# Attention scores from one stacked product of 96 rows instead of three products with a block-diagonal operand

## The reference

```python
x = x + attn(lstm(x, cond))        # LSTM over 128 steps, then causal attention, 16 heads, latent keys of 32
x = x + moe(gru(x, cond))          # GRU over 128 steps (a projection after every 4th), then 8 experts, top 2

# attention, with h the LSTM's output:
q      = einsum('bld,dhk->blhk', h, Wq)
latent = h @ Wkv_down                                  # [.., 32]
k, v   = latent @ Wk_up, latent @ Wv_up
a      = softmax(where(mask, q @ k.T / sqrt(64), min))
y      = (a @ v) @ Wout
```

## Time and profile before

| | |
|---|---|
| median of 3 runs | 546.38 us (544.72 to 546.54) |
| the profiled execution | 542.14 us, its span 540.4 us |
| TensorE busy | 508.1 us, 94% (7464 products) |
| VectorE busy | 435.9 us, 81% |
| ScalarE busy | 364.7 us, 67% |
| GpSimd busy | 34.6 us, 6% |
| query transfers | 256 of 16 KB, median 1.9 us from issue to landing |
| granted TensorE clock | 0.971 of full speed |

### The profile page before, as it was taken

One profiled execution on the slowest core, in us unless ns is written; L12 is line 12 of the kernel. 1 busy time (PEld: TensorE's weight loads), 2 busy tenths in 40 slices (PEclk: granted clock), 3 DMA queues, 4 the chain that ended last, 5 costly groups with the idle time before them and its releaser, 6 DMA issues.

```text
span 540.4 us, 20477 instructions
## 1 busy us (share of the span) xinstructions
PE 508.1 (94%) x7464; PEld 468.7 (87%) x7506; DVE 435.9 (81%) x2370; ACT 364.7 (67%) x1329; POOL 34.6 (6%) x89
## 2 busy tenths in 40 slices
PE   7988889898799999999999999999999999889997
PEld 3756666898689999999999999999999998879986
DVE  4567888789878888888888888898888888865785
ACT  2355645875467767677777777676767677776995
POOL 7000010100000000001010101010000001000010
PEclk9799999999769999999999999999999999979999
DMA  8910102010101011110101010101010111100000
GB/s 212 366 18 7 20 2 23 2 19 11 21 3 16 9 15 16 16 12 12 19 14 16 7 18 15 21 3 19 15 16 8 14 16 16 12 1 1 13 6 13
DMA packets 75121, 14.35 MB, mean 27 GB/s; under 512 B 71412, under 2 KB 74112, under 8 KB 74639
## 3 DMA queue, kind: packets, MB, share of 16 engines
q1 hardware_dynamic: 74566, 11.96, 12.3%
q10 hardware_dynamic: 456, 1.08, 0.7%
HBM read 7.78 MB, written 1.05 MB: 16 GB/s over the span
## 4 chain that ended last, share of the span: by engine, by line
PE 78%; DVE 10%; ACT 6%; issue 4%; SPq 1%; DMA 1%; POOL 0%; ACTq 0%; DVEq 0%; POOLq 0%
PE pH L516 19%; PE pY L516 13%; PE pG L516 12%; PE pL L516 9%; PE pC L516 7%; PE pV L516 7%; PE pC L608 6%; PE pS L516 5%; ACT hid L912 2%; ACT PThi L901 1%; SPq L436 1%; DVE w1lo L1189 1%; DVE ghi L1233 1%; DMA gscale<-in_gscale 1%; ACT P L895 1%
## 5 line engine op out<-in xcount | busy, mean ns | idle before, releaser
L912 ACT ACTIVATE hid<-pH,b 128x256 f32<-128x256 f32 (+1 forms) x320 | 115.1, 449 | 0.0
L516 PE MATMUL pY<-w,hid 128*128 128x128 f32 (+1 forms) x656 | 80.9, 268 | 0.0
L516 PE MATMUL pH<-ghi,w1hi 128*128 128x256 f16 (+1 forms) x320 | 76.0, 254 | 2.3 <-ACT hid L912 1.7
L516 PE MATMUL pH<-ghi,w1lo 128*128 128x256 f16 (+1 forms) x320 | 76.3, 255 | 0.0
L516 PE MATMUL pH<-glo,w1hi 128*128 128x256 f16 (+1 forms) x320 | 76.3, 255 | 0.0
L516 PEld LDWEIGHTS pY<-w,hid 128*128 128x128 f32 (+1 forms) x656 | 70.5, 171 | 0.1
L923 ACT ACTIVATE gT<-pG 128x32 f32<-128x32 f32 x128 | 24.9, 194 | 54.8 <-PE pG L516 52.8
L901 ACT ACTIVATE PThi<-pC 128x512 f16<-128x512 f32 x64 | 38.1, 596 | 22.0 <-PE pC L608 21.8
L516 PE MATMUL pG<-gRZ,gW 128*128 128x16 f32 x256 | 45.6, 254 | 4.2 <-DVE gRZ L1206 3.9
L516 PEld LDWEIGHTS pG<-gRZ,gW 128*128 128x128 f32 x256 | 40.0, 196 | 8.0 <-DVE gRZ L1206 6.8
L516 PEld LDWEIGHTS pL<-hhi,lWhi 128*128 128x128 f16 x512 | 42.1, 116 | 5.4 <-DVE hhi L1250 4.6
(11 more groups left out here) (188 smaller groups left out, 1641.0 us busy)
## 6 DMA issues: line engine op xcount, KB each, us to landing
w<-in_w SPq DMA_DIRECT2D x2, 2048.0 KB, 13.7
qbd<-qh SPq DMA_DIRECT2D x256, 16.0 KB, 1.9
out<-acc SPq DMA_DIRECT2D x16, 64.0 KB, 1.6
xT<-in_xT ACTq DMA_DIRECT2D x1, 960.0 KB, 7.9
hid<-in_WqT SPq DMA_DIRECT2D x1, 512.0 KB, 5.4
hid<-in_Wout SPq DMA_DIRECT2D x1, 512.0 KB, 9.9
lWh<-in_lWh SPq DMA_DIRECT2D x1, 256.0 KB, 2.8
lWx<-in_lWx SPq DMA_DIRECT2D x1, 256.0 KB, 3.3
```

Source lines behind the costliest of these rows:

```text
L516: return nc.tensor.matmul(o, lhsT=lhsT, rhs=rhs, start=start, stop=stop, skip_group_check=True)
L912: A(hid[:, e % NHID, c, 0:W], pH[half][:, W * at:W * (at + 1)], ACT.Gelu, bias=b1[:, e, c:c + 1], scale=1.0 / SP).then_inc(gelu, 1)
```

## The change

The three products of a sequence become one. The high and low queries and a second copy of the high queries are stacked in 96 partitions of a new tile `qst` (rows 0 to 31 high, 32 to 63 low, 64 to 95 high again), and the latents in `latst` (rows 0 to 63 `lathi`, 64 to 95 `latlo`), so that one product over 96 rows gives the same sum. No row of another head group is in it, so nothing is block-diagonal and nothing need be cleared. `qst` has two buffers, by period.

SP fills rows 0 to 63 by 8 transfers of 32 KB for each period, four from the high part and four from the low part. Rows 64 to 95 are filled by copies on the engines, in the step after the queries: two of 32x512 on ScalarE, two on VectorE. GpSimd makes two more copies a period, of 64x128 and 32x128, for `latst`. The query tile `qh` has its high and low halves apart instead of interleaved by sequence.

```diff
-            def spread_queries(n):
-                p, u = divmod(n, NU)
-                if u == 0:
-                    sp.wait_ge(q_lo, p + 1)
-                if n == 0:
-                    sp.wait_ge(cleared, NCLEAR)
-                if n >= 2:
-                    sp.wait_ge(s_mm, n - 1)
-                for q in range(HQ):
-                    r = slice(32 * q, 32 * q + 32)
-                    sp.dma_start(qbd[r, n % 2, :, :, q, :]..., qh[r, p % 2, 4 * u:4 * u + 4, :, :, :]...).then_inc(qbd_done[n % 2], 16)
+            def spread_queries(p):
+                for r, l, ready in ((0, 0, q_hi), (1, 1, q_lo)):
+                    sp.wait_ge(ready, p + 1)
+                    if p >= 2 and r == 0:
+                        sp.wait_ge(s_mm, NU * (p - 1))
+                    for q in range(HQ):
+                        sp.dma_start(qst[LD * r:LD * (r + 1), p % 2, :, 32 * q:32 * q + 32],
+                                     qh[32 * q:32 * q + 32, p % 2, l, :, :, :]...).then_inc(qst_done[p % 2], 16)
...
+                if latents_at(k - 1) is not None:          # SP, at the head of its step k
+                    spread_queries(latents_at(k - 1))
...
                 pool.wait_ge(lat_split, 2 * G + 2)
+                pool.tensor_copy(latst[0:2 * LD, :, c], lathi[0:2 * LD, :, c]).then_inc(lat_stack, 1)
+                pool.wait_ge(lat_stack, 2 * G + 1)
+                pool.tensor_copy(latst[2 * LD:3 * LD, :, c], latlo[2 * LD:3 * LD, :, c]).then_inc(lat_stack, 1)
+                pool.wait_ge(lat_stack, 2 * G + 2)
...
-                pe.wait_ge(lat_split, 2 * (p + 1))
-                pe.wait_ge(qbd_done[n % 2], 16 * HQ * (n // 2 + 1))
+                pe.wait_ge(lat_stack, 2 * (p + 1))
+                pe.wait_ge(qst_done[p % 2], 16 * 2 * HQ * (p // 2 + 1))
+                pe.wait_ge(qst_dup, 2 * (p + 1))
+                pe.wait_ge(qst_dup2, 2 * (p + 1))
...
-                    mm(S, flat(qbd[:, n % 2, j, 0, :, :]), lathi[:, b, 0:L])
-                    mm(S, flat(qbd[:, n % 2, j, 0, :, :]), latlo[:, b, 0:L])
-                    last = mm(S, flat(qbd[:, n % 2, j, 1, :, :]), lathi[:, b, 0:L])
+                    last = mm(S4[:, j, :], qst[:, p % 2, b, :], latst[:, b, 0:L])
...
+            def q_again(p, q):                             # ScalarE
+                act.wait_ge(q_hi, p + 1)
+                if p >= 2 and q == 0:
+                    act.wait_ge(s_mm, NU * (p - 1))
+                A(qst[2 * LD:3 * LD, p % 2, :, 32 * q:32 * q + 32], qh[32 * q:32 * q + 32, p % 2, 0, :, :, :]..., ACT.Copy).then_inc(qst_dup, 1)
...
+                if latents_at(k - 1) is not None:          # ScalarE, behind the experts' activations, ahead of gp
+                    q_again(latents_at(k - 1), 0)
...
+                if latents_at(k - 1) is not None:          # ScalarE, behind lC
+                    q_again(latents_at(k - 1), 1)
...
+            def q_again(p):                                # VectorE
+                if p >= 2:
+                    dve.wait_ge(s_mm, NU * (p - 1))
+                for q in range(2, HQ):
+                    V.tensor_copy(qst[2 * LD:3 * LD, p % 2, :, 32 * q:32 * q + 32],
+                                  qh[32 * q:32 * q + 32, p % 2, 0, :, :, :]...).then_inc(qst_dup2, 1)
...
+                if latents_at(k - 1) is not None:          # VectorE, behind hlo, at the end of step k
+                    q_again(latents_at(k - 1))
```

More of the change, by code:

```diff
@@ L240, in build @@
         latlo = sb("latlo", [128, B, T], f16)
+        latst = sb("latst", [3 * LD, B, T], f16)
         latNhi = sb("latNhi", [128, B, LD + 1], f16)
         latNlo = sb("latNlo", [128, B, LD + 1], f16)
-        qh = sb("qh", [128, 2, B, 2, HG, TB], f16)
-        qbd = sb("qbd", [128, 2, 4, 2, HQ, 32], f16)
+        qh = sb("qh", [128, 2, 2, B, HG, TB], f16)
+        qst = sb("qst", [3 * LD, 2, B, H * TB], f16)
         mx = sb("mx", [128, 2, 4])
@@ L343, in build @@
         lat_split = sem("lat_split")
+        lat_stack = sem("lat_stack")
+        qst_dup = sem("qst_dup")
+        qst_dup2 = sem("qst_dup2")
         latn_done = sem("latn_done")
@@ L347, in build @@
         q_lo = sem("q_lo")
-        qbd_done = [sem(f"qbd_done{n}") for n in range(2)]
+        qst_done = [sem(f"qst_done{n}") for n in range(2)]
         s_mm = sem("s_mm")
@@ L386, in build @@
         HALVES = (0.5, 1.0)
-        NCLEAR = 12
+        NCLEAR = 11
         PARTS = (0, 64, 96)
@@ L424, in _ @@
                 sp.dma_start(whole(t), a[name]).then_inc(loaded_moe, 16)
[L426 to L437 removed]
+            def spread_queries(p):
[5 more added lines that the diff above has]
+                        sp.dma_start(qst[LD * r:LD * (r + 1), p % 2, :, 32 * q:32 * q + 32],
+                                     qh[32 * q:32 * q + 32, p % 2, l, :, :, :].rearrange("p b g t -> p b (g t)")).then_inc(qst_done[p % 2], 16)
             def store(i):
@@ L445, in _ @@
             for k in range(STEPS + 2):
[L446 to L450, removed]
+                if latents_at(k - 1) is not None:
+                    spread_queries(latents_at(k - 1))
                 for i in range(NG):
@@ L477, in _ @@
             pool.memset(g8[:, T + 1, :], SH / 2).then_inc(cleared, 1)
-            assert NCLEAR == 12
+            assert NCLEAR == 11
             pool.memset(whole(onesP), 0.0).then_inc(set_ones, 1)
@@ L881, in q_copy @@
                 if p >= 2:
-                    for half in range(2):
-                        act.wait_ge(qbd_done[half], 16 * HQ * NU // 2 * (p - 1))
-                A(qh[:, p % 2, :, 0, :, :], pC[:, :].rearrange("p (g s b) -> p b g s", g=HG, b=B),
+                    act.wait_ge(qst_done[p % 2], 16 * 2 * HQ * (p // 2))
+                    act.wait_ge(qst_dup2, 2 * (p - 1))
+                A(qh[:, p % 2, 0, :, :, :], pC[:, :].rearrange("p (g s b) -> p b g s", g=HG, b=B),
                   ACT.Copy, scale=1.0 / SP).then_inc(q_hi, 1)
+            def q_again(p, q):
+                act.wait_ge(q_hi, p + 1)
+                if p >= 2 and q == 0:
+                    act.wait_ge(s_mm, NU * (p - 1))
+                A(qst[2 * LD:3 * LD, p % 2, :, 32 * q:32 * q + 32], qh[32 * q:32 * q + 32, p % 2, 0, :, :, :].rearrange("p b g t -> p b (g t)"),
+                  ACT.Copy).then_inc(qst_dup, 1)
             def exps(n):
@@ L1031, in q_rest @@
                 dve.wait_ge(q_hi, p + 1)
-                V.scalar_tensor_tensor(qh[:, p % 2, :, 1, :, :],
+                V.scalar_tensor_tensor(qh[:, p % 2, 1, :, :, :],
                                        pC[:, :].rearrange("p (g s b) -> p b g s", g=HG, b=B), 1.0 / SP,
-                                       qh[:, p % 2, :, 0, :, :], ALU.mult, ALU.subtract).then_inc(q_lo, 1)
+                                       qh[:, p % 2, 0, :, :, :], ALU.mult, ALU.subtract).then_inc(q_lo, 1)
             def turn_latents(p, whole_t, turned):
@@ L1042, in turn_latents @@
                 V.transpose(turned[rows, :, 0:LD], whole_t[rows, :, 32 * j:32 * j + 32]).then_inc(latn_done, 1)
+            def q_again(p):
[3 more added lines that the diff above has]
+                    V.tensor_copy(qst[2 * LD:3 * LD, p % 2, :, 32 * q:32 * q + 32],
+                                  qh[32 * q:32 * q + 32, p % 2, 0, :, :, :].rearrange("p b g t -> p b (g t)")).then_inc(qst_dup2, 1)
             def maximum(n):
```

2 lines of the change are left out of this document (removed).

## The result

| | runs | median us | lowest to highest | profiled run | its span | mean clock |
|---|---|---|---|---|---|---|
| before | 20 | 543.43 | 541.10 to 548.13 | 542.14 | 540.4 | 0.971 |
| after | 20 | 546.53 | 543.94 to 548.73 | 547.39 | 545.5 | 0.969 |

The ratio of the two is 1.0062, with a 95% interval of 1.0046 to 1.0078: the change makes the kernel 2.5 to 4.2 us slower. The absolute time is the one forecast (546.5), but that is partly luck. The median of before that was shown came from 3 runs, and over 20 it lies 3 us lower. The forecast change was +0.1 us; the measured one is +3.4, just past the half per cent that I had set as the bound of "no change".

The account below looks back on a forecast made before the run. Bounds: TensorE busy 94% of the span, VectorE 81%. Terms -7.1 + 5.0 + 1.9 + 1.8 - 1.1 - 0.4 = +0.1 us gave 542.2 us profiled, 546.5 carried to the runs' median; 8-in-10 range 541 to 560.

Parts of the forecast that it names:

- score products, ten steady periods: TensorE, periods 5 to 14: removing 8 of each unit's 12 products saves 3.9 plus 3.2 us, -7.1 us.
- VectorE's and ScalarE's copies, steady: Step after the queries: VectorE's two cost 0.5 us a period, 5.0 over ten; ScalarE's two hide in idle time, 0.
- transfers, steady: SP's eight transfers before unit 0: last lands at 6.7 or 7.4 us, TensorE comes at 7.5, so 0.
- to period 5, all: Periods 0 to 4: transfers +1.9 us, copies less covered by idle time +1.8, shorter units -1.1.
- last period: End of the kernel: both recurrences no longer fill TensorE, -0.4 us.
- two thirds of a score product's time reaches the end: Steady periods: they grow 3.9 us while units grow 5.7; the other third falls into TensorE's waits.
- VectorE's copies: Two 32x512 copies between `hlo` and `gRZ`: 0.42 us each, 0.92 with gaps, 0.56 beyond the idle time.
- The estimate of 0.29 us that stood beside the sum: VectorE copy at four elements a cycle, by the Trainium skill: excess 0.3 us a period, sum below 2 us lower.
- Rival (a): Copies cheap (VectorE's excess 0 to 0.3 us a period), saving passes: -2 to -8 us, about 541 us; chance 0.22.
- So in the steady periods it is hidden with 0.1 to 0.8 us left: 0.: Before unit 0: the last transfer lands 6.7 to 7.4 us after the high queries, TensorE arrives at 7.5; no cost.
- Rival (b): Last of eight transfers becomes the wait before unit 0, issues 0.85 or 1.2 us apart: 557 or near 594 us; chance 0.20.
- In period 0 the forecast: Unit 0 of period 0: transfers not hidden, data land at 36.8 us, the wait grows by 1.7 us.

Follow-up runs that it names:

- x1: Kernel before with one of the three score products of a sequence, the other two left out, all else as before; 538.26 us, ratio 0.9905.
- x6: Kernel after without SP's transfers, the wait for them and the four engine copies; stacked latents and the 96-row product stay; 537.73 us, ratio 0.9898.
- x5: Kernel before with the four 32x512 copies (two ScalarE, two VectorE) added into a tile nobody reads; 544.68 us, ratio 1.0036.
- x3: Kernel after without SP's eight transfers a period and TensorE's wait for them; the copies stay; 542.57 us, ratio 0.9979 to before.
- y2: Kernel after, unchanged, run again for a second profile; 547.89 us (one run).
- z1: Kernel after with the four low transfers issued by GpSimd, the four high ones still by SP; 542.21 us, ratio 0.9981 to before.
- x2: Kernel after without the four engine copies; the transfers and TensorE's wait for them stay; 544.13 us, ratio 1.0016 to before.

## Why the prediction was right or wrong

The profiles of before and after differ by 545.5 - 540.4 = 5.1 us, of which the steady part holds 1.9, the part to period 5 4.6, the rest -1.5 (and the first copy starts 0.1 later). By the steps of the prediction:

| step | forecast | measured | read from |
|---|---|---|---|
| score products, ten steady periods | -7.1 | -4.1, -3.5 | x1, x6 against before |
| VectorE's and ScalarE's copies, steady | +5.0 | +0.8 | x5 - before, x3 - x6 |
| transfers, steady | 0 | +4.5 (y2: +3.4) | after - z1, after - x3 |
| to period 5, all | +2.6 | +4.6, +4.3 | both pairs |
| last period | -0.4 | -1.5 | after - before |

**The products: right in kind, too large.** The term "two thirds of a score product's time reaches the end" took all growth of the periods for TensorE's. x1 has one product where there were three, and its steady periods still grow, from 28.08 to 28.48 us. Other things widen with the same columns: from period 0 to 15 VectorE's maximum over the scores goes from 182 ns to 679, and ScalarE's exponentials from 272 to 369 each. Before, the steady periods grow by 0.83 us, so about 0.4 us of that is the two removed products'. An experiment that a kernel makes on itself varies all that depends on the variable.

**VectorE's copies: mis-sized, on the safe side.** 0.42 us came from a slope of 0.52 ns an element of a CAST with four-byte input. The copy takes 0.286:

VectorE and ScalarE of the kernel after in period 7, in the step after the queries; it answers to the earlier trace rows.

```profile
231.65 0.17 DVE L1270 TENSOR_TENSOR hlo<-hfull,hhi 128x16 f16<-128x16 f32 x1
231.85 0.60 DVE L1058 COPY qst<-qh 32x512 f16<-32x512 f16 x2
232.49 0.19 DVE L1223 SCALAR_TENSOR_TENSOR gRZ<-gT,g 128x32 f32<-128x32 f32 x1
```

```profile
230.31 0.63 ACT L890 ACTIVATE qst<-qh 32x512 f16<-32x512 f16 x1
231.02 0.18 ACT L965 ACTIVATE g<-pG 128x16 f32<-128x16 f32 x1
231.10 0.21 ACT L968 ACTIVATE lC<-lT 128x16 f32<-128x16 f32 x1
231.33 0.63 ACT L890 ACTIVATE qst<-qh 32x512 f16<-32x512 f16 x1
232.03 0.20 ACT L929 ACTIVATE gT<-pG 128x32 f32<-128x32 f32 x1
```

The estimate of 0.29 us that stood beside the sum, from VectorE: DVE Perf Modes of the Trainium skill, is what came, for two-byte SBUF tiles with inner runs of 32 elements. So of 0.36 us idle time and 0.60 us of copies only 0.24 was excess: `gRZ` of period 7 starts 5.51 us after the high-query copy's end in x3 and 5.26 in x6. A third of that reached the end: 0.08 us a period. ScalarE's two copies lie in the idle times in which they were put; the `gT` behind them starts 5.06 us after the copy's end in x3 and 5.03 in x6, so they cost next to nothing in the steady part. Rival (a) had this price right and the saving of the products too large: without the transfers' wait the steady part is 2.7 us below before.

**The transfers: the step that failed.** "So in the steady periods it is hidden with 0.1 to 0.8 us left: 0." Issue distance, landing, last landing (7.0 us against 6.7) and TensorE's arrival all came nearly as forecast in the periods that nothing disturbs. What failed is that I priced a margin of 0.1 to 0.8 us at nothing. Even that margin was mis-added: with one issue of 1.8 us in place of 0.65 the last transfer lands 4.55 + 1.15 + 2.1 = 7.8 us after the high queries, not 7.4, and that is behind TensorE's 7.5; the 4.0 us that a landing can take stood in the earlier trace rows, too. Rival (b) named the wait but wanted every issue to be slower. It came in the periods with an instruction fetch among the transfers, eight of ten, and z1 and x3 show what it cost. In period 0 the forecast held: landing at 36.8 us forecast, 37.3 measured, the wait longer by 1.7 us forecast and 1.46 measured.

**The early part: 2 us too low, and open.** x1, x5, x2, x3 and z1, each with a different part of the change, all take 137.0 to 138.2 us up to period 5, before and x6 134.3 to 134.9. That is most of the 5.1 us between the two profiles, and z1 has only 1.5 of it less. Period 4 alone lasts 29.2 to 30.6 us in all of these and in x6, and 28.4 and 28.6 in the two profiles of before. Low stretches of the clock are not all of it: x5 has none between 30 and 140 us and still takes 3.0 us more than before. One execution each can't settle it.

Adding up: -5.1 (x1) + 2.0 (x5) + 4.3 (after less z1) = +1.2 us, against +3.4 measured, with about 1 us of uncertainty on each. Part of the rest is that prices depend on what stands beside them: the same four copies cost 2.0 us beside three products and 4.8 us in x3 against x6, though 0.8 in the steady part of both; the difference lies in the early part. The forecast of a gain and prices that nearly cancel was right; which price cancels it was wrong. In the steady part I took the saving of the products 3.6 us too high, the copies 4.2 too high and the transfers 4.5 too low. That errors of this size left the total so near was luck.

## What to carry to other kernels

Where a change turns "the first of many transfers is needed" into "the last of many is needed", compare the margin with the longest issue and the longest landing in the trace, not with their medians, and look for instruction fetches in the window; issuing from a second queue bought back all of it in the steady part here (z1). Fewer products only pay as far as TensorE ends the step, and a self-made slope overstates this when other engines' work grows with the same variable. The sum for an edit is best checked at each margin that it leaves below 1 us, since these are what the next execution disturbs.

## What the runs showed of the hardware

- With twice the runs an issue on SP's queue takes hardly longer: 629 ns with 512 runs of 64 B, 611 ns with 256.
- A transfer issued from GpSimd takes it 648 ns. With six on each of two queues, landing takes a median of 3.1 us and at most 6.1; with eight on one queue 2.1 and 3.6.
- One 16 KB instruction packet takes a DMA engine 1.0 to 1.5 us in the steady part of the kernel after. Where one falls among the transfers, the last of them lands 0.3 to 1.7 us later than the 6.95 us of an undisturbed period.
- A GpSimd copy of 32x512 two-byte elements takes 615 ns, against 286 on VectorE and 627 on ScalarE. VectorE operations with two SBUF inputs that start beside it are held until its end (`lT<-lP` from a mean of 174 ns to one of 570).
- Products of 96 rows follow each other as those of 128 do, 0.028 us apart at 64 columns; alternating ones of 64 and 32 rows stand 0.13 us apart.
